# Reordering the head of a graph-attention and expert kernel: first weight chunks ahead of the bias rows, and a new order of VectorE's work in the normalisation loop

## What is computed

```python
# T = 2048 tokens, D = 512, 8 experts, F = 1024, top 2
xn = layernorm(x)                                  # (x - mean) / sqrt(var + 1e-5), per row
q, k, v = xn @ W_q.T + b_q, xn @ W_k.T + b_k, xn @ W_v.T + b_v
z = (q @ k.T) / sqrt(D) * adj
z = where(z == 0, -10000, z)
x = x + relu(softmax(z, axis=1) @ v)
y = layernorm(x)
w = softmax over the two largest of softmax(y @ Wr)   # placed in 8 columns
out = x + swiglu(y; shared) + sum_e w[:, e] * swiglu(y; expert e)
```

## Time and profile before

| | us |
|---|---|
| median of 3 runs | 1374.59 |
| lowest and highest run | 1374.21, 1377.01 |
| the profiled execution, its own time | 1377.3 |
| its span in the trace | 1375.6 |
| PE busy in the span | 1365.6 (99%) |
| DVE, ACT, POOL busy | 909.2, 453.6, 196.9 |
| granted TensorE clock, mean | 0.998 of full |

### The profile page before, as it was taken

The page is one execution under the profiler, slowest core; times in us unless marked ns, Lnnn a source line. Parts: engine busy times, 40 slices in busy tenths (PEclk is TensorE's granted clock), DMA queues, the critical chain, the costliest instruction groups (busy, mean ns, idle before and its releaser), DMA issues.

```text
span 1375.6 us, 19783 instructions
## 1 busy us (share of the span) xinstructions
PE 1365.6 (99%) x6720; PEld 1177.3 (86%) x6720; DVE 909.2 (66%) x1957; ACT 453.6 (33%) x702; POOL 196.9 (14%) x234
## 2 busy tenths in 40 slices
PE   9999999999999999999999999999999999999998
PEld 7888888888888878898989889898898989888887
DVE  7957767767777767465576747566475736367874
ACT  4522212212212245342343424234242525243331
POOL 3500112212211321011011110201102020100000
PEclk9999999999999999999999999999999999999999
DMA  5916565466466564462616133361435252553101
GB/s 183 259 46 169 163 185 165 148 187 168 153 175 191 175 237 147 154 175 55 206 31 215 31 106 124 54 207 34 124 107 152 83 155 98 148 151 107 47 16 61
DMA packets 114420, 185.47 MB, mean 135 GB/s; under 512 B 13776, under 2 KB 47568, under 8 KB 114336
## 3 DMA queue, kind: packets, MB, share of 16 engines
q1 hardware_dynamic: 98064, 153.43, 35.5%
q0 software_dynamic: 9760, 18.93, 7.0%
q10 hardware_dynamic: 6528, 12.22, 3.1%
HBM read 129.82 MB, written 55.77 MB: 135 GB/s over the span
## 4 chain that ended last, share of the span: by engine, by line
PE 91%; DVE 3%; DMA 3%; issue 2%; ACT 1%; SPq 0%; POOL 0%; DVEq 0%; ACTq 0%; POOLq 0%
PE bank L307 83%; PE bank L1042 5%; DMA turned<-p_moved 1%; DMA p_moved<-turned 1%; PE bank L874 1%; PE bank L1033 1%; DMA early_x<-x2t 0%; ACT sc L1210 0%; PE bank L798 0%; PE bank L752 0%; DVE fill L1602 0%; DVE pT_l L1457 0%; PE bank L868 0%; DVE turned L1620 0%; SPq L459 0%
## 5 line engine op out<-in xcount | busy, mean ns | idle before, releaser
L1846 DVE TENSOR_TENSOR hid<-bank,hid 128x384 f32<-128x384 f32 (+1 forms) x80 | 46.8, 584 | 176.6 <-PE bank L307 176.4
L307 PE MATMUL bank<-dn_h,hT_h 128*128 128x512 f32 x320 | 125.7, 393 | 0.2 <-DVE hT_l L1457 0.2
L307 PE MATMUL bank<-dn_h,hT_l 128*128 128x512 f32 x320 | 125.7, 393 | 0.0
L307 PE MATMUL bank<-dn_l,hT_h 128*128 128x512 f32 x320 | 125.6, 392 | 0.0
L307 PE MATMUL bank<-xq_h,gate_h 128*128 128x384 f32 (+1 forms) x320 | 111.3, 348 | 0.1
L307 PE MATMUL bank<-xq_h,gate_l 128*128 128x384 f32 (+1 forms) x320 | 111.2, 348 | 0.0
L307 PE MATMUL bank<-xq_l,gate_h 128*128 128x384 f32 (+1 forms) x320 | 110.8, 346 | 0.0
L307 PE MATMUL bank<-xq_h,up_h 128*128 128x384 f32 (+1 forms) x320 | 110.7, 346 | 0.0
L307 PE MATMUL bank<-xq_h,up_l 128*128 128x384 f32 (+1 forms) x320 | 110.4, 345 | 0.0
L307 PE MATMUL bank<-xq_l,up_h 128*128 128x384 f32 (+1 forms) x320 | 110.4, 345 | 0.0
L1128 ACT ACTIVATE hT_h<-hid 128x384 fp32r<-128x384 f32 (+1 forms) x96 | 53.8, 561 | 164.2 <-DVE hid L1846 124.7
(11 more groups left out here) (278 smaller groups left out, 3294.8 us busy)
## 6 DMA issues: line engine op xcount, KB each, us to landing
gate_raw<-in_L_ffn_Wg_dram SPq DMA_DIRECT2D x16, 1024.0 KB, 5.5
up_raw<-in_L_ffn_Wu_dram SPq DMA_DIRECT2D x16, 1024.0 KB, 10.2
dn_raw<-in_L_ffn_Wd_dram SPq DMA_DIRECT2D x16, 1024.0 KB, 12.5
sc<-in_adj_dram SPq DMA_DIRECT2D x30, 512.0 KB, 6.1
p_moved<-turned SPq DMA_DIRECT2D x30, 512.0 KB, 3.0
turned<-p_moved SPq DMA_DIRECT2D x120, 128.0 KB, 5.4
x_t<-in_x_dram SPq DMA_DIRECT2D x24, 256.0 KB, 4.8
slots<-x2row ACTq DMA_DIRECT2D x12, 512.0 KB, 4.4
```

What stands on the lines that cost most here:

```text
L307: mm = pe.matmul(o, lhs(a, c), rhs(b, c), start=first and n == 1, stop=last and n == 3 * len(chunks))
L1846: dve.tensor_tensor(hid[:, c % 2, 0:w], bank[2 + c % 2][:, 0:w], hid[:, c % 2, 0:w], ALU.mult).then_inc(sem("hid"), 1)
```

## The change

The change touches the head and the normalisation loop and nothing else:

- SP issues the first chunks of `W_q` and `W_k` ahead of the two bias rows.
- DVE does the low parts of those two chunks ahead of the spreading of `b_k`; the waits for POOL's set-up and for the bias rows move with it.
- PE makes 12 matmuls of zeros in place of 14, and has `A_part(o)` ahead of `c2_part(o)`; `c2_part(2)` and `c2_part(3)` now follow each other.
- On DVE `layer_norm(2)`, `inputs(1)` and `measure(3)` stand ahead of the four `c1` reductions.
- In DVE's loop the order is `values(t-1)`, `layer_norm(t+2)`, `inputs(t+1)`, `measure(t+3)`.
- DVE's `values(12)` and `values(13)` wait for `layer_norm(14)` and `layer_norm(15)`, since `v_l` of these tiles lies over the buffers `x_late`. Both stand ahead of them in DVE's order.

```diff
-        WARM = 14
+        WARM = 12
...
-            sp.dma_start(bqk[:, 0, :], b_q.rearrange("(p c) -> p c", c=DC)).then_inc(sem("in_b"), 16)
-            sp.dma_start(bqk[:, 1, :], b_k.rearrange("(p c) -> p c", c=DC)).then_inc(sem("in_b"), 16)
             for c in range(DC):
                 for raw, w, name in ((wq_raw, w_q, "wq"), (wk_raw, w_k, "wk")):
                     sp.dma_start(raw[:, c, :], w.rearrange("(p c) n -> p c n", c=DC)[:, c, :]).then_inc(sem(f"in_{name}{c}"), 16)
+                if c == 0:
+                    sp.dma_start(bqk[:, 0, :], b_q.rearrange("(p c) -> p c", c=DC)).then_inc(sem("in_b"), 16)
+                    sp.dma_start(bqk[:, 1, :], b_k.rearrange("(p c) -> p c", c=DC)).then_inc(sem("in_b"), 16)
...
+            A_part(0)
             c2_part(0)
-            A_part(0)
+            A_part(1)
             c2_part(1)
-            A_part(1)
+            A_part(2)
             c2_part(2)
-            A_part(2)
             c2_part(3)
...
-            dve.wait_ge(sem("setup"), SETUP["triangle"])
-            dve.wait_ge(sem("in_b"), 32)
-
...
-            replicated(bk, 1, 0)
             for c in range(DC):
                 for w, raw, name in ((wq, wq_raw, "wq"), (wk, wk_raw, "wk")):
                     dve.wait_ge(sem(f"{name}_h"), c + 1)
                     minus(w["l"][:, c, :], raw[:, c, :], w["h"][:, c, :]).then_inc(sem(f"{name}_l"), 1)
+                if c == 0:
+                    dve.wait_ge(sem("setup"), SETUP["triangle"])
+                    dve.wait_ge(sem("in_b"), 32)
+                    replicated(bk, 1, 0)
...
+                if NT - 4 <= t < NT - 2:
+
+                    dve.wait_ge(sem("ln1_done"), t + 3)
                 minus(v["l"][:, t, :], bank[2 + t % 2][:], v["h"][:, t, :]).then_inc(sem("v_l"), 1)
...
             A_chunk(3)
+            layer_norm(2)
+            inputs(1)
+            measure(3)
             dve.wait_ge(sem("bias_ps"), 2)
...
             dve.tensor_copy(bb[:], bank[5][:, 0:1]).then_inc(sem("bias_read"), 1)
-            inputs(1)
...
-            for t in range(NT):
+            for t in range(1, NT):
+                values(t - 1)
                 if t + 2 < NT:
                     layer_norm(t + 2)
+                if t < NT - 1:
+                    inputs(t + 1)
                 if t + 3 < NT:
                     measure(t + 3)
-                if 0 < t < NT - 1:
-                    inputs(t + 1)
-                if t > 0:
-                    values(t - 1)
```

## The result

The changed kernel takes 1381.3 us (median of 18 runs, 1378.91 to 1385.55). The kernel before, run beside it on the same chips, took 1377.18 (median of 18, 1374.21 to 1380.87; the 1374.59 that the prediction started from was the median of the first three of these). The ratio is 1.0032, 95% interval 1.0024 to 1.0040: +4.4 us, between +3.3 and +5.5. **Slower**, by a third of a per cent, which is clear of the noise: +4.4 where +3.5 was forecast. The absolute time lies above the stated range (1371.6 to 1379.7).

The account below looks back on a forecast made before the run. PE bounds the kernel before; reordered, DVE's ring through POOL bounds the loop. Gains of 0.38 + 0.46 + 1.89 against 0.57 lost a tile leave +3.5: 1374.59 + 3.5 = 1378.1 us, own range 1376.8 to 1379.3, whole 1371.6 to 1379.7.

Parts of the forecast that it names:

- The ring: DVE's loop, tied to POOL: `xn` stands still until `spent` ends, `xnT_l` comes after; 3.77 us a turn against PE's 3.20.
- T: In DVE's loop, the end of a `var_e`; `xn` was forecast to start at about T + 0.77, `spent` at T + 0.60.
- The entry: Start of the loop: PE's waits ahead of `turn_input(2)` and `values(2)` go, gaining 0.46 and 1.89 us.
- The head: Kernel start: twelve matmuls of zeros and an earlier first chunk let PE start at 6.40 in place of 6.78, gaining 0.38 us.
- Rival 3: Head gives nothing: the first chunk lands as before, PE starts at 7.29, all shifts; 1379.0 us, chance 0.05.
- The sum: At the loop's end: `turn_input(15)` at 76.31 in place of 72.79, +3.5 us in all; nothing counted behind the loop.
- The base: Whole kernel: the +3.5 us was added to the median of runs, 1374.59 us, taken as good to +-0.5.
- The waits of PE in the loop: In the loop: some 20 short waits of PE, 0.2 to 0.3 us each, for `xn` and `xnT_l` in turn.
- Rivals 1 and 2: DVE's loop: rival 1, `xn` runs beside `spent` at 0.54, 1371.9 us, chance 0.16; rival 2, some turns only, 1373.4, 0.09.
- rival 2: DVE's loop: now and then `xn` is first and makes `spent` wait; with every second turn 1373.4 us, chance 0.09.

Follow-up runs that it names:

- the slow ring: Changed kernel, its repeat, and the kernel before with only DVE's loop reordered; against before 1.0032, 1.0031 and 1.0045.

## Why the prediction was right or wrong

- **The ring: right, in kind and size.** 3.77 us a turn forecast, (74.50 - 33.01) / 11 = 3.77 measured. `xn` 1.41 and 1.40. The start of `xn` at T + 0.77, from one row at 30.95, came out at 37.55 - 36.78 = 0.77.
- **The entry: right.** PE's waits ahead of `turn_input(2)` and `values(2)` are gone. `xn` of tile 3 was forecast to be blocked to 31.02; it ran from 30.80 to 31.42, 0.62 us, and ended 0.28 behind its `spent` (31.14). The `var_e` of tile 4 ended at 33.01 and not 32.62, as much later as the head's missing 0.38. The gain of the entry by itself came out smaller than its two waits together, since with the old loop the wait for `v_l` of tile 0 only shrinks; the prediction hadn't separated the two.
- **The head: the step that failed in the trace.** "Twelve leave PE free for the next at 6.33" took the rise of the clock behind the ninth matmul as a property of the kernel. In this execution all twelve came some 0.43 us apart (5.39 us in all), as 512 columns do at 1.2 GHz, the lower of the clock's two levels, and PE was free at 6.77. `wk_l` was ready at 6.31, as forecast (6.33). The term was -0.38 and measured 0.0 here; for the head alone the gain was 0.16 to 0.31 at `turn_input(15)`. Rival 3 (1379.0) had the same sign by another cause, a late landing, which didn't happen: `wq_h` started at 4.36, forecast 4.33.
- **The sum** became +3.94 in place of +3.52 at `turn_input(15)`, nearly all of the 0.42 from the head's term. The span grew by 3.5, the forecast number, and that is luck: the part behind the scores' first matmul happened to be 0.5 shorter (1290.6 and 1291.1).
- **The base: the step that put the time outside the range.** I added the sum to a median of three runs, 1374.59, and gave that +-0.5. The same kernel had a median of 1377.18 over 18 runs. The 2.7 us by which the profiled execution (1377.3) stood above the median of three was the sign, and I used it the wrong way: two of four executions were at 1377, and the range should have been wide enough for the base to be there. On three single chips the median of before was 1376.8, 1376.8 and 1377.9. The granted clock goes with it: on one chip the runs of before with a mean of 1.000 had a median of 1375.7 us (eight runs) and those with 0.998 one of 1377.4 (six). The profiled execution had 0.998. From 1377.18, +3.5 is 1380.7 against 1381.3. The measured 4.4 (3.3 to 5.5) holds the forecast 3.5.
- **The waits of PE in the loop** were forecast as some 20 rows of 0.2 to 0.3 us. The list of waits gives three, of 0.5 us together. The loss is real, but it is recorded as something else (below).
- **Rivals 1 and 2** fell: in the three profiles of the slow ring all 37 `xn` of it started behind their `spent` and took 1.40 or 1.41 us. That an `xn` which is first makes `spent` wait, on which rival 2 leaned, is shown by no run: where `xn` is first, in the kernel with `spent` behind `xn`, a semaphore keeps the two apart.

## What to carry to other kernels

When an engine's loop is in step with another engine, write down the ring of dependences from one turn to the next before reordering it: work that stands in the shadow of a wait is free, and the same work on the other side of that wait is paid in full on each turn. Here 0.60 us moved across one instruction cost 5.0 us net by the end of the loop. Moving the other low part into the shadow as well, or letting the blocked instruction go first, turned the loss into a gain of 0.13 to 0.15% against before, entry and head included. And set the sum of a small change on the widest base of runs there is; a median of three was off by more than half of the effect.

## What the runs showed of the hardware

- A VectorE `tensor_scalar` from SBUF to SBUF that meets a GpSimd `tensor_tensor` ends 0.27 to 0.29 us behind it, for GpSimd instructions of 1.29 and of 0.74 us and for starts from 0.16 to 0.96 us into them. An `xn` alone takes 0.54, so about half of its own length passes before the GpSimd instruction is over: one that met only the last 0.34 us of `spent` took 0.62 in all, not 0.34 + 0.54. Which part runs early the traces don't show. The Trainium skill ("SBUF — State Buffer", "Who interferes with whom") says that a VectorE instruction in a mode that uses two ports, which `tensor_scalar` can enter, and a GpSimd instruction never share: the one that comes second fully blocks. In these traces GpSimd was always first, and no `xn` ended before the `spent` that it met; that `xn` ran in such a mode, and the case of VectorE first, they don't show. `tensor_tensor` with one operand in PSUM and the statistics beside the same GpSimd instruction kept their 0.68 us.
- PE's short waits hide in its busy time. Between 40 and 70 us the kernel before and the changed one (start and end, length, busy and count, clock):

```profile
40.00:70.00 30.00, 30.00 (x154) 1.00 0.87 250
```
```profile
40.00:70.00 30.00, 28.87 (x129) 1.00 0.86 228
```

  25 matmuls fewer fit into the stretch, a sixth, and busy time fell by 1.13 us of 30. Matmuls are recorded 0.39 us long at a distance of 0.23, so a gap shorter than the 0.16 by which a record outlasts that distance doesn't show as idle. Counts in a window, or the distance of the same instruction from turn to turn, tell it; the busy share and the list of waits don't.
- The rise of PE's clock at the start differs between executions of the same head by up to 1 us over twelve matmuls (4.40 to 5.39), and the time behind the scores' first matmul, some 1290 us, by 5.7 us between twelve profiles (1288.3 to 1294.0). In part that is a fall of the granted clock near 490 us, which nine executions had and three had not. A difference of 0.1% in one profile's span is no evidence of a difference between kernels.
